# SP's order of transfers in an attention pipeline: k's parts and stack, then q's, then the shift rows

## What is computed

```
x = x + tanh(g_xattn) * attention(layernorm(x), ctx, ctx)     # 16 heads of 16 dims, rope on q and k
x = x + tanh(g_ffn)   * ffn(layernorm(x))                     # quantised, 768 hidden dims

scores = q @ k.T / sqrt(16), where |query - key| <= 50, else -1e9
out    = softmax(scores) @ v
```

## Time and profile before

| | |
|---|---|
| median of 3 runs | 1407.23 us (1406.34 to 1412.29) |
| the profiled execution | 1405.53 us, its span 1403.8 us |
| mean granted clock of TensorE | 0.941 of full speed |
| PE, DVE, ACT, POOL busy | 85%, 86%, 60%, 42% of the span |
| DMA packets | 207.27 MB, 148 GB/s over the span |
| one transfer of k's or q's parts to DRAM | 384 KB, median 2.6 us from issue to landing |

### The profile page before, as it was taken

The page is one execution under the profiler, slowest core; times in us unless marked ns, Lnnn a source line. Parts: engine busy times, 40 slices in busy tenths (PEclk is TensorE's granted clock), DMA queues, the critical chain, the costliest instruction groups (busy, mean ns, idle before and its releaser), DMA issues. The chain is left out here.

```text
span 1403.8 us, 27833 instructions
## 1 busy us (share of the span) xinstructions
PE 1195.9 (85%) x8960; PEld 807.6 (58%) x8992; DVE 1202.3 (86%) x3570; ACT 837.5 (60%) x1336; POOL 587.1 (42%) x1392
## 2 busy tenths in 40 slices
PE   3367898988888888888888767999899979977998
PEld 2245676776766766666676543444333334436887
DVE  5678998999999899899989736998899989997886
ACT  2225665656666565657565545664676779993332
POOL 1127787778778787778777640000000000000000
PEclk7679999999999999999999988999999999998999
DMA  3174856566666667575757311222455455556774
GB/s 113 34 161 108 180 137 159 137 159 148 149 157 149 153 144 158 138 158 139 169 127 170 85 38 45 112 91 111 151 188 187 170 179 193 188 179 203 234 237 164
DMA packets 132369, 207.27 MB, mean 148 GB/s; under 512 B 11159, under 2 KB 97050, under 8 KB 126106
## 3 DMA queue, kind: packets, MB, share of 16 engines
q1 hardware_dynamic: 132250, 205.86, 53.6%
HBM read 125.60 MB, written 79.69 MB: 146 GB/s over the span
## 5 line engine op out<-in xcount | busy, mean ns | idle before, releaser
L596 ACT ACTIVATE probs<-psum 128x356 f32<-128x356 f32 x512 | 210.2, 464 | 246.4 <-PE psum L852 246.4
L707 DVE CUSTOM_DVE_ANT_0 psum<-psum,band 128x178 f32<-128x178 f32 x1024 | 317.2, 372 | 40.1 <-PE psum L835 38.5
L1014 PE MATMUL psum<-xnT,w_upT 128*128 (+1 forms) x1152 | 260.8, 384 | 19.1 <-DVE maxima L1238 8.8
L527 POOL TENSOR_SCALAR_AFFINE_SELECT probs<-probs 128x154 f32<-128x154 f32 (+1 forms) x512 | 214.3, 426 | 146.9 <-ACT probs L596 141.0
L835 PE MATMUL psum<-k_stack,q_stack 96*128 96x178 bf16 x1024 | 143.2, 251 | 88.0 <-issue 57.2
L1014 PEld LDWEIGHTS psum<-xnT,w_upT 128*128 128x128 f16 x1152 | 109.7, 99 | 170.0 <-issue 32.2
L536 POOL TENSOR_SCALAR_AFFINE_SELECT probs<-probs 128x254 f32<-128x254 f32 (+1 forms) x512 | 189.1, 393 | 0.0
L835 PEld LDWEIGHTS psum<-k_stack,q_stack 96*128 96x128 bf16 x1024 | 76.5, 100 | 145.4 <-issue 86.6
L707 DVE DVE_READ_ACCUMULATOR2_ANT smax<- 128x1 f32 x1024 | 142.7, 139 | 0.0
L1614 PE MATMUL psum<-w_downT,xnT 128*128 128x256 f16 x1152 | 128.1, 275 | 16.0 <-DVE xnT L1564 16.0
L1014 PE MATMUL psum<-xnT,w_gateT 128*128 (+1 forms) x576 | 125.9, 382 | 8.7 <-DVE xnT L1087 8.7
(11 more groups left out here) (189 smaller groups left out, 2283.7 us busy)
## 6 DMA issues: line engine op xcount, KB each, us to landing
k_parts_scratch<-k_parts SPq DMA_DIRECT2D x32, 384.0 KB, 2.6
q_parts_scratch<-q_parts SPq DMA_DIRECT2D x32, 384.0 KB, 2.6
k_stack<-k_parts_scratch SPq DMA_DIRECT2D x32, 384.0 KB, 5.1
q_stack<-q_parts_scratch SPq DMA_DIRECT2D x32, 384.0 KB, 6.0
gate_scratch<-g_stage SPq DMA_DIRECT2D x16, 768.0 KB, 3.3
g_in<-gate_scratch SPq DMA_DIRECT2D x16, 768.0 KB, 4.6
sig_scratch<-w_gateT SPq DMA_DIRECT2D x32, 384.0 KB, 2.3
sig_again<-sig_scratch SPq DMA_DIRECT2D x32, 384.0 KB, 3.4
```

The lines of the kernel that those rows point to most:

```text
L527: nc.gpsimd.affine_select(out=t[:, :, 0:n], in_=t[:, :, 0:n], pattern=[[0, 2], [1, n]], compare_op=ALU.is_ge, fill=0.0, base=WINDOW - off, ...
L596: nc.scalar.activation(ring_tile(probs, b, pair, c)[:].rearrange("p e j -> p (e j)"), scoreT_bank[c][:, 0:2 * SPAN], ACT.Exp, scale=DK ** ...
L707: ins = nc.vector.tensor_tensor_reduce(out=mine, in0=mine, in1=keep["band"][:, t, :], scale=1.0, scalar=-3e38, op0=ALU.add, op1=ALU.max, a ...
L1014: last = nc.tensor.matmul(bank[:], weights[wp][:, c * I + f * P:c * I + (f + 1) * P], x_parts[:, c, bass.ds(j * (2 * TILE) + xp * TILE, TI ...
```

## The change

SP's list of a step is put into another order. Nothing is added or removed, and no other engine's list is touched.

```diff
             def steps(rnd, unit):
-                load_shift(Batch(rnd, unit, 2), 0)
-                load_stacks(Batch(rnd, unit, 1), "q")
                 load_x(Batch(rnd, unit, -1))
                 store_x2(Batch(rnd, unit, 4))
                 load_residual(Batch(rnd, unit, 3))
                 load_shift(Batch(rnd, unit, 2), 1)
-                store_parts(Batch(rnd, unit, 0), "k")
-                store_parts(Batch(rnd, unit, 0), "q")
-                load_stacks(Batch(rnd, unit, 0), "k")
+                for n in "kq":
+                    store_parts(Batch(rnd, unit, 0), n)
+                    load_stacks(Batch(rnd, unit, 0), n)
+                load_shift(Batch(rnd, unit, 1), 0)
```

## The result

The changed kernel takes 1446.49 us (median of 4 runs, 1440.21 to 1453.69) against 1408.14 us before (median of 4): a ratio of **1.027, 95% interval 1.0216 to 1.0323, slower**. The forecast was 1395.7 us, and the range ended at 1417.

What follows compares the result with a forecast made beforehand. PE's wait for q's stack, capped by DVE's hole, was taken as the bound. Transfer terms summed to 16.5 us against 16.95 and 17.91; 27 x 0.45 = 12 us gained, edges costing 0.5, gave 1395.7 us, range 1380 to 1417.

Steps and rivals of the forecast that it cites:

- Whose landing ends PE's wait: PE before scores: q's stack ends its wait now, the shift rows after, with a hole some 1.1 us long.
- k's stack early, q's store in line behind it: SP's queue: k's loads start at S + 2.65, not S + 5.26; q's store lands 0.9 us behind them.
- The two loads on an empty queue: SP's loads of k's and q's stacks: 6.0 us each, bounds 5.0 to 7.2 and 4.4 to 8.2.
- S: The moment in a step at which SP issues the store of k's parts; the forecast counts times from it.
- "These edits cost nothing" for the later shift rows: Later shift rows and x loads in SP's queue: no cost beyond the sum; ACT's exponentials shift by 1 us.
- DVE's hole is the cap: Each step gains only the smaller of PE's advance and DVE's hole; DVE's whole wait is 0.8 us per step.
- The edges, "about 0.5 us": First three batches and the last, outside the 27 steps: losses and gains together cost about 0.5 us.
- "Slower decides at 17.4 from S to first scores": Slower rival, chance 0.19: decided by S to first scores above 17.4 us, the mean of the two steps read.
- the rival's 1446 us: Slower rival, chance 0.19: strictly serial transfers ahead of q's loads cost 1.3 us per step; 1446 us, or 1427 with half.

Runs made afterwards that it cites:

- k_first: Changed kernel with half 0 of the shift rows put back ahead of q's stack, k's stack still ahead of q's store: 1414.89 us, ratio 1.0049.
- swap_before: Kernel before, transfers untouched, but PE runs pair 0's transposed scores behind its plain scores: 1454.3 us, ratio 1.0325.
- q_before_shift: Kernel before with only q's stack moved ahead of half 0 of the shift rows; q's store stays ahead of k's stack: 1447.34 us, ratio 1.0269.
- split_k: Kernel before with the first of k's three loads put ahead of q's store, shift rows still ahead of q's stack: 1381.62 us, ratio 0.9793.
- swap_q_before_shift: q_before_shift, but PE runs pair 0's transposed scores behind its plain scores: 1450.61 us, ratio 1.0291.
- split_k_q_first: split_k with q's stack put ahead of half 0 of the shift rows: 1396.72 us, ratio 0.9895.
- fill_hole: Changed kernel with 8 extra unused matmuls on PE ahead of its wait for half 0 of the shift rows: 1433.28 us, ratio 1.0168.

## Why the prediction was wrong

- *Whose landing ends PE's wait*: right; q's stack in the kernel before, the shift rows in the changed one, with the hole ahead of the transposed scores as described.
- *k's stack early, q's store in line behind it*: right in kind. The store follows k's landing by 1.1 us (0.9 charged), and by 0.9 from ACT's queue.
- *The two loads on an empty queue*: **the first step that failed, by its size**. I took 6.0 us each, because the queue is empty; they took 7.0 (k; bounds 5.0 and 7.2) and 7.1 (q; bounds 4.4 and 8.2). Nothing moves for at least the first 1.1 us, as the window from k's issue shows:

```profile
436.03:437.20 1.17, 0.82 (x7) 0.26 (x5) 1.10 (x9) 1.17 (x4) 1.17 (x5) 1.00 0.00 0
```

  The lower bound had been counted from the landing of a store ahead, in which this start and the first bytes were hidden. These 2.1 us are the whole of the sum's error: 18.6 us from S to the plain scores against 16.5. The gain foreseen ahead of the plain scores, 0.9 us against 17.4, becomes a loss of 0.9 against 17.8, the mean of all 27 steps (the two that I had read give 17.4). k_first has the same long loads and keeps the shift rows ahead: it starts the plain scores at 17.8 and is even, so this size takes away the gain and doesn't make the loss alone.
- *"These edits cost nothing" for the later shift rows*: **the second step that failed, and it was no matter of size**. The sum charged 0.9 us for them ahead of the plain scores (0.5 and 0.4), and the changed kernel is 0.9 behind k_first there; that was right. But it put at nothing what comes behind them. I let the exponentials slip with a line on ACT's 60% and priced only PE's wait. From the plain scores to the next S the step is 0.6 us longer in the changed kernel and 1.4 in swap_before; with both parts, 2.5 to 2.9 us of lateness of the transposed scores cost 1.3 to 1.7 us per step in q_before_shift and swap_before. ACT is idle over 40% of the span, and still its exponentials hold up PE's next pairs, and through them DVE.
- *The clock*: left out of the sum. A step has 3.3 us at the half clock instead of 1.4. Filling the hole gave back 13 us of 38 in the changed kernel and 7 of 39 in q_before_shift.
- *DVE's hole is the cap*: right where the transposed scores stay in place. split_k takes away DVE's whole wait for the plain scores, 0.8 us per step, and its step is 0.8 us shorter.
- *The edges, "about 0.5 us"*: wrong; the first four items lose 8.0 us. In the first two q's store lands at S + 10.1 and 10.3 instead of 5.5 and 5.6, and the plain scores start at S + 17.0 and 18.6, where I had 16.0 and 16.5.
- *"Slower decides at 17.4 from S to first scores"*: not the deciding quantity. k_first is at 17.8 and even, swap_q_before_shift is at 17.7 and 3% slower. Nor do the transposed scores decide alone: split_k_q_first has them 1.0 us later than the kernel before and is 1% faster. DVE's idle time counts both. That the rival's 1446 us is what was measured is partly luck: it had 1.3 us per step ahead of the plain scores and 4 us at the start, where 0.9, a further 0.6 behind them, and 8.0 were measured.

Left open: how the 0.6 us behind the plain scores splits between the half clock and the wait for the exponentials (fill_hole takes away most of the one, no run takes away the other), and whether the clock falls by the hole's place or its length. That a later store is why filling gives back less in q_before_shift is read from the profiles; no run tests it.

## What to carry to other kernels

When a transfer is moved back in a queue, find the first instruction that needs it and the time at which it runs now, and then read what every engine has queued behind that instruction's results: here an engine that was 60% busy still had no slack at that place. Then sum up the holes of the engine with the least idle time, place by place: in this kernel they gave each step's length. A load that starts on an empty queue isn't to be priced by how soon a queued one ends behind the bytes ahead of it: queued, k's and q's loads ended 5.3 and 4.4 us after the transfer ahead had landed, on an empty queue they took 7.0 and 7.1 us. So overlap them: let one transfer of the next chain go ahead of the store that you wait for, not all of them. And test a suspected dependency by moving the instruction alone, with all transfers left in place.

## What was not expected of the hardware

A store issued by ACT on its own queue moved none of its 384 KB until the loads that SP had issued before it were all but done, and landed after 5.5 us (median) as from SP's queue, against 2.6 us in the kernel before. And 1.3 us of unused matmuls per step made the kernel before 1% faster, with the granted clock going from 0.97 to 1.00 between 160 and 780 us.
